# Experts over 13 tiles of 128 tokens instead of 14 of 112, two per-token values spread over the channels by DMA, and a new order of the work

## The reference

```
y   = layernorm over channels (x)                       # per token: (x - mean) * rstd
y   = spatial gate(y) * y                               # theta, phi, gram, joint, hidden, logit, sigmoid
y   = channel gate(y) * y                               # three products with 784-wide weights, gram, joint, sigmoid
x   = x + y
t   = x as tokens; tn = layernorm(t)
p   = softmax(tn @ router_w + router_b); top 2 of 8 experts, renormalised
t   = t + sum over the 2 of p_k * (tn @ expert_w[k] + expert_b[k])
out = t back as images
```

## Time and profile before

| | us |
|---|---|
| median of 3 runs | 2124.07 (2121.37 to 2126.17) |
| profiled execution, its own time | 2119.73 |
| its span, first to last instruction | 2117.9 |
| TensorE busy | 1966.1 |
| VectorE busy | 1602.6 |
| ScalarE busy | 1182.8 |
| GpSimd busy | 1041.1 |

### The profile page before, as it was taken

How to read it: one execution, slowest core, us unless ns; L and a number is a source line. 1 busy time by engine, 2 the same in 40 slices (tenths; PEclk the granted TensorE clock), 3 DMA queues, 4 the chain that set the end, 5 groups by cost and what they waited for, 6 DMA issues and landing times.

```text
span 2117.9 us, 41604 instructions
## 1 busy us (share of the span) xinstructions
PE 1966.1 (93%) x14484; PEld 1425.6 (67%) x14484; DVE 1602.6 (76%) x4919; ACT 1182.8 (56%) x3304; POOL 1041.1 (49%) x1233
## 2 busy tenths in 40 slices
PE   1689999999999999999999999999999999999986
PEld 1466677776677676667777667777666776766663
DVE  2457787887778787778788877878877788887775
ACT  1346555565655556665556565555666555556534
POOL 0225545555454554554455555455554545555544
PEclk9899999999999999999999999999999999999998
DMA  3000000000000000000000000000000000000000
GB/s 101 1 17 24 24 31 16 32 32 24 32 24 32 17 32 28 27 24 32 19 29 32 24 32 24 32 16 32 32 24 32 24 32 17 31 24 32 9 16 31
DMA packets 23707, 57.78 MB, mean 27 GB/s; under 512 B 5132, under 2 KB 6333, under 8 KB 23502
## 3 DMA queue, kind: packets, MB, share of 16 engines
q1 hardware_dynamic: 23502, 55.13, 7.4%
HBM read 29.43 MB, written 25.69 MB: 26 GB/s over the span
## 4 chain that ended last, share of the span: by engine, by line
PE 63%; DVE 18%; issue 12%; ACT 5%; SPq 1%; POOL 1%; DMA 0%; DVEq 0%; POOLq 0%; ACTq 0%
DVE part L1419 5%; PE high L1019 5%; ACT part L625 5%; PE rot L771 5%; PE low L1019 4%; PE rot L844 4%; PE high L1021 4%; PE rot L824 4%; PE high L1020 4%; PE low L1021 4%; PE low L1020 3%; PE rot L763 3%; PE rot L756 3%; PE rot L857 2%; PE rot L794 2%
## 5 line engine op out<-in xcount | busy, mean ns | idle before, releaser
L625 ACT ACTIVATE part<-low,gv 112x128 f32<-112x128 f32 x1792 | 500.9, 392 | 277.8 <-issue 134.3
L426 POOL TENSOR_TENSOR part<-part 112x256 f32<-112x256 f32 x448 | 344.8, 770 | 474.5 <-DVE part L1419 474.2
L1419 DVE SCALAR_TENSOR_TENSOR part<-high,gv,part 112x128 f32<-112x128 f32 x1792 | 493.7, 342 | 110.5 <-ACT part L625 97.4
L888 PE MATMUL rot<-x1h,wch 112*128 112x256 f32 x1120 | 280.9, 289 | 6.5 <-ACT x1h L564 6.5
L889 PE MATMUL rot<-x1h,wcl 112*128 112x256 f32 x1120 | 269.4, 279 | 0.0
L431 POOL TENSOR_TENSOR otok<-part 112x128 f32<-112x128 f32 x448 | 208.0, 464 | 35.1
L417 POOL TENSOR_TENSOR x1l<-tok,x1h 112x1024 fp32r<-112x1024 f32 x64 | 135.7, 2121 | 175.3 <-ACT x1h L564 175.3
L1019 PE MATMUL low<-weh,xh 128*112 128x512 f32 x448 | 196.8, 439 | 25.7 <-ACT part L625 23.1
L888 PEld LDWEIGHTS rot<-x1h,wch 112*128 112x128 f32 x1120 | 211.6, 189 | 12.9 <-ACT x1h L564 12.6
L889 PEld LDWEIGHTS rot<-x1h,wcl 112*128 112x128 f32 x1120 | 211.9, 189 | 0.0
L387 POOL TENSOR_TENSOR rstd<-var,mhalf 112x14 f32<-112x14 f32 x32 | 85.2, 2662 | 255.1 <-DVE var L1219 255.1
(11 more groups left out here) (204 smaller groups left out, 3903.6 us busy)
## 6 DMA issues: line engine op xcount, KB each, us to landing
xin<-in_x SPq DMA_DIRECT2D x32, 784.0 KB, 4.3
out<-x SPq DMA_DIRECT2D x64, 392.0 KB, 2.3
otok<-in_ggs_w SPq DMA_DIRECT2D x1, 600.2 KB
y_ch<-in_ggs_w SPq DMA_DIRECT2D x1, 600.2 KB
j<-in_expert_w SPq DMA_DIRECT2D x1, 512.0 KB
x<-in_thc_w SPq DMA_DIRECT2D x1, 392.0 KB
x<-in_phc_w SPq DMA_DIRECT2D x1, 392.0 KB
x<-in_gxc_w SPq DMA_DIRECT2D x2, 183.8 KB
```

The costliest lines, as they stand in the source:

```text
L426: nc.gpsimd.tensor_tensor(part[:, slot, 0:2, :], part[:, slot, 0:2, :], part[:, slot, 2:4, :], ALU.add).then_inc(sem("half_sum"), 1)
L625: last = nc.scalar.activation(part[:, slot, e, :], low[i % 2][0:T, e * C:(e + 1) * C], ACT.Copy, scale=gv[o][:, i, e:e + 1])
L888: nc.tensor.matmul(dst, wch[:, j, rows], hi_x, start=(j == 0), stop=False)
L1419: last = nc.vector.scalar_tensor_tensor(out=part[:, slot, e, :], in0=high[i % 2][0:T, e * C:(e + 1) * C], scalar=gv[o][:, i, HALF + e:HALF ...
```

## The change

**Tiles.** The second half cuts a pair's 1568 tokens without regard to the border of the images: 12 tiles of 128 tokens and one of 32 (`TILES` is 13), in four pieces of three, three, three and four tiles (`FLAT`). Statistics, shift, routing, gates, expert halves, token sums and `finish` all go by these tiles and pieces. The first half keeps its tiles of 112. An expert tile's PSUM bank and its slot in `part` now go by a running count over all pairs, since 13 is odd.

**Spreading by DMA.** Instead of 14 transposes of a broadcast column, one transpose turns the values of all tiles to rows (14 x 112 or 13 x 128), ScalarE copies them to SBUF, SP writes them to a row in DRAM, waits for that, and reads the row back into all 128 partitions of `y_ch` or `cen`. `normalise` and `centre` then work in place: both operands lie in SBUF.

**Order.** The lists of all engines, and `USES`, are new. Among others `mixed` and its copies move to the next step (back 1), `x_tokens`, `stats1`, `moments1` and `centre_tokens` move to the early part of the step, nine tiles of gating (4 to 12) come ahead of `x1_tokens`, `normalise` comes right behind `x1_tokens`, and the routing behind that.

```diff
+TILES = -(-PAIR * S // 128)
+FLAT = ((0, 3), (3, 6), (6, 9), (9, TILES))
...
+                def row_out(name, src, back):
+                    if live(k, p, back):
+                        need(sp, f"{name}_row_ready", k, p, 1, back)
+                        sp.dma_start(rows_dram[name][turn(back) % 2], src[:, :]).then_inc(sem(f"{name}_row_out"), 16)
+                def row_in(name, dst, back):
+                    if live(k, p, back):
+                        sp.wait_ge(sem(f"{name}_row_out"), 16 * (turn(back) + 1))
+                        sp.dma_start(dst, rows_dram[name][turn(back) % 2].rearrange("i t -> (i t)")[0:PAIR * S].partition_broadcast(128))\
+                          .then_inc(sem(f"{name}_spread"), 16)
...
                 load(0)
+                shift_out(2)
+                shift_in(2)
+                rstd_out(0)
+                rstd_in(0)
                 store(0, 3)
                 store(1, 3)
...
+                def rstd_turn(back):
+                    if live(k, p, back):
+                        free(pe, "rstd_row", k, p)
                         need(pe, "rstd1_ready", k, p, 1, back)
-                        spread(f"scale{b}{q}", rstd1[par(p, back)], b, q, back).then_inc(sem("scale_filled"), 1)
+                        nc.tensor.transpose(bank("rstd_row", k, p, back)[0:2 * NT, 0:T], rstd1[par(p, back)][:, :], ident[0:T, 0:T])\
+                            .then_inc(sem("rstd_row_filled"), 1)
...
-                        need(dve, "scale_filled", k, p, 2 * b + q + 1, back)
-                        nc.vector.tensor_tensor(y_ch[:, b, cols(q)], bank(f"scale{b}{q}", k, p, back)[:, 0:width(q)],
-                                                x[par(p, back)][:, b, cols(q)], ALU.mult).then_inc(sem("y_ch_ready"), 1)
+                        dve.wait_ge(sem("rstd_spread"), 16 * (2 * k + p - back + 1))
+                        own = y_ch[:, b, cols(q)]
+                        nc.vector.tensor_tensor(own, own, x[par(p, back)][:, b, cols(q)], ALU.mult).then_inc(sem("y_ch_ready"), 1)
...
+                def centre(f, back):
+                    if live(k, p, back):
+                        dve.wait_ge(sem("shift_spread"), 16 * (2 * k + p - back + 1))
+                        own = flat(cen)[:, span(f)]
+                        nc.vector.tensor_tensor(own, flat(x2[par(p, back)])[:, span(f)], own, ALU.subtract)\
                             .then_inc(sem("centred_ready"), 1)
```

More of the change, by code:

```diff
@@ L229, in need, with rows, span, flat @@
             eng.wait_ge(sem(name), k * (2 * PER[name]) + ((p - back) * PER[name] + n))
+        def rows(i):
+            return min(128, PAIR * S - 128 * i)
+        def span(f):
+            return slice(128 * FLAT[f][0], min(128 * FLAT[f][1], PAIR * S))
+        def flat(v):
+            return v[:, :, :].rearrange("p b s -> p (b s)")
+        def piece(i):
+            return min(i // 3, 3)
+        def count_of(k, p, back, i):
+            return (2 * k + p - back) * TILES + i
         def ago(i, d, back):
@@ L1006, in router, with finish @@
                         last.then_inc(sem("rlogit_filled"), 1)
-                def finish(b, q, back):
+                def finish(f, back):
                     if live(k, p, back):
-                        free(pe, f"fin{b}{q}", k, p)
-                        need(pe, "token_ready", k, p, NT * b + QUART[q][1], back)
-                        to_channels(f"fin{b}{q}", otok, b, q, back).then_inc(sem("fin_filled"), 1)
-                def products(dst, o, i, half):
-                    b, j = i // NT, i % NT
-                    tile = slice(j * T, (j + 1) * T)
+                        free(pe, f"fin{f}", k, p)
+                        need(pe, "token_ready", k, p, FLAT[f][1], back)
+                        for i in range(*FLAT[f]):
+                            n = rows(i)
+                            last = nc.tensor.transpose(bank(f"fin{f}", k, p, back)[:, (i - FLAT[f][0]) * 128:][:, 0:n],
+                                                       otok[0:n, i, :], ident[0:n, 0:n])
+                        last.then_inc(sem("fin_filled"), 1)
@@ L1046, in step @@
+                low_half(7, 3)
+                high_half(6, 3)
+                high_half(7, 3)
+                mixed(1)
+                x_tokens(0, 0, 0)
+                x_tokens(0, 1, 0)
+                x_tokens(1, 0, 0)
+                x_tokens(1, 1, 0)
+                high_half(8, 3)
                 joint(0, 0, 1)
-                x2_tokens(1, 1, 2)
-                low_half(7, 3)
-                high_half(7, 3)
+                joint(0, 1, 1)
+                high_half(9, 3)
+                finish(1, 3)
@@ L1097, in step @@
                 high_half(3, 2)
+                gram_first(1)
+                tp_tokens(0, 0)
+                low_half(2, 2)
+                gram_turn(1)
+                channels(2, 1)
                 joint_c(1)
-                scale(1, 0, 0)
-                scale(1, 1, 0)
                 high_half(4, 2)
                 hidden_c(1)
-                theta_phi(0, 0)
-                finish(0, 0, 2)
+                finish(0, 2)
+                low_half(3, 2)
+                channel_logit(1)
@@ L1441, in step @@
+                stats2(3, 2)
+                gate_high(6, 3)
+                moments2(2)
+                mix_low(1)
+                gate_high(7, 3)
+                stats1(0, 0)
+                shifts(2)
+                stats1(1, 0)
+                finish(1, 3)
+                moments1(0)
                 gate_high(8, 3)
+                centre_tokens(0, 0)
                 gate_high(9, 3)
-                shifts(2)
                 gate_high(10, 3)
-                centre(0, 0, 2)
-                centre(0, 1, 2)
```

503 lines of the change are left out of this document (247 added, 256 removed).

## The result

The changed kernel takes 2187.3 us (median of four runs, 2185.3 to 2190.1) against 2125.1 for the kernel before on the same chip: ratio 1.0295, 95% interval 1.0278 to 1.0312. Slower, as forecast and inside the range, but by 62 us where the forecast had 21.

The account below looks back on a forecast made before the run. TensorE bounds the kernel before; after the change a closed VectorE-TensorE circle does: 31.0 + 26.9 + 5.0 = 62.9 us a step against 62.44. 2119.7 + 13 (29 steps) + 12 (filling and draining) = 2145 us, range 2045 to 2190.

Parts of the forecast that it names:

- The closed chain: VectorE's new order and TensorE's channel products wait on each other in one circle; the step can't be shorter, 62.9 us.
- C: Circle from residual(1,1) to the first x1h: 29.6 us of work plus 1.3 of blocking by GpSimd, 31.0 (rounded up).
- A: Circle from channels0_high to the channel logit: 23.3 us work, 0.5 small waits, 3.1 waiting for normalise behind x1_low; 26.9.
- B: Circle from the channel logit to residual(1,1): one tile of gating, the gate and four residuals on VectorE, 5.0 us.
- What TensorE saves: Spreading transposes 2.99 us less 0.3, 14th tile 1.4, logits and token transpose 0.1: 4.2 a step, leaving 56.4.
- The first line of "what would show it": Normalise (448 columns) well above 0.55 us, its third piece ending 4 us or more after x1h(0).
- The second: Sign in the profile after: TensorE waits for normalise before theta_phi(0), about 3 us a step.
- The trips through DRAM: Each spread takes 6.6 us out and in, hidden under 8.9 us of cover for the shift, 10.6 for the deviation.
- Rival 3: The spread from one DRAM row is slow, 11 us out and in: step 65.0, 2214 us; chance 0.06.
- Filling: Uncovered trips at the start, 6.6 us each for the first pair's deviation and shift, within +12 for filling and draining.
- The draining: At the end, some 3 us in each of the two last shifts; about 7 credited for the saved tile and transposes.
- Rival 1: TensorE stays the bound, faster, 2056 us, if blocking in A and C together is below about 3.6 us; chance 0.37.

Follow-up runs that it names:

- hold_x1: The changed kernel with GpSimd's x1_low held until both x1_tokens are done: 2242.4 us, 1.0572 of the kernel before.
- no_x1low: The changed kernel with x1_low working on 8 columns only from the second pair on, leaving out the fine part of x1: 2074.7 us, 0.978 of the kernel before.
- tiles_only: The kernel before with only the 13 tiles of 128 tokens added, spreads still by TensorE transposes and lists in the old order: 2066.3 us, 0.9747.
- warm: The changed kernel with 22 unused matmuls of 256 columns a step filling TensorE's gap in channels0_high: 2154.0 us, 1.0151 of the kernel before.
- pool_after: hold_y with GpSimd's x_low(1) to x_low(3) moved behind x1_low, and gx(1) ahead of channels0_low on TensorE: 2183.4 us, 1.0291 of the kernel before.
- rstd_twice: The changed kernel with the DMA spread of the reciprocal deviation read twice, one after the other: 2195.1 us, 1.0353 of the kernel before.
- dma_old_order: 13 tiles and both spreads by DMA as in the change, but lists in the order of the kernel before: 2517.4 us, 1.1863 of that kernel.
- hold_y: The changed kernel with x1_low held until both x1_tokens and all of normalise are done: 2181.8 us, 1.0292 of the kernel before.
- swap_low: The changed kernel with x_low(3) ahead of add_token(12) in GpSimd's list: 2195.8 us, 1.0347 of the kernel before.
- split_low: The changed kernel with each x1_low issued as four and three instructions, back to back: 2209.1 us (two runs), 1.04 of the kernel before.

## Why the prediction was right in sign and wrong in size

**The closed chain: right.** No engine is the bound (TensorE 88%, VectorE 73%), and the step follows what lies on the circle: longer in hold_x1 (66.0), shorter in no_x1low (60.4). The parts, measured on the same marks: C 30.2 us (residual(1,1) ends at 1029.3, x1h(0) at 1059.5) for 31.0; A 28.4 (to the channel logit) for 26.9; B 5.35 for 5.0. Sum 63.95 for 62.9.

**What TensorE saves: right for the tile (1.5 us, tiles_only), too high in all.** It works 57.5 us a step in no_x1low where I had 56.4. tiles_only, with its spreads by transposes, has 59.1, so the two spreads gave back some 1.6 us where the sum had 2.7.

**Part C: near, by two errors.** centre lost less than the 1.3 assumed: 731 ns for 384 columns against 546 from PSUM in tiles_only, three times, 0.55 in all. GpSimd paid instead, x_low at 1344 ns against 1012. And "VectorE without waits from the statistics of x2 to the space gate" was wrong: it waits 0.89 us for ScalarE at 1045.5, and the chain of waits in the changed kernel runs over TensorE and ScalarE up to 1047.4 and over VectorE only from there.

**Part A is the step that failed.** The prediction put the block on normalise: "GpSimd is released to x1_low(0)" at the instant when VectorE is free for it, 3.1 us. It had VectorE free there "since x1_tokens(1) runs beside that copy", that is at its 0.95 us. The row of 2391 ns for this form was read as one GpSimd instruction's rest, and it was: before, GpSimd had x1_low(0) and then a gap. In the new list add_token(12) and x_low(3) run straight into x1_low(0), and x1_tokens(1) took 4.56 us; TensorE waited in channels0_high, 2.7 us, and normalise was free. By itself this wait is no longer than the one forecast. What was missing from the sum is what TensorE does after it: theta_phi(0) and gx(0) at half clock, 1.0 us in their two groups and 1.2 a step in all, about 31 us of the kernel (warm). This is the term that was put at nothing without a reason. The prediction had the clock at 1.00 throughout, as the earlier trace rows shows it, and did not ask what a wait of 3 us does to it. Without the term its step comes out: 62.7 us in warm, and 62.6 to 62.7 in the changed kernel's five full-clock steps, for 62.9 forecast. The first line of "what would show it" thus came out wrong: normalise takes 0.61 us, and its third piece ends 5.4 us after x1h(0) only because it starts late. The second came out nearly (2.7 us of wait, before another group), the third too (share 88% for 89, rest 5.2 us for 6.5).

The rule of the Trainium skill that the prediction weighed (SBUF — State Buffer, Who interferes with whom) says that a VectorE instruction with two SBUF inputs contends with a GpSimd instruction that reads SBUF. The trace agrees on x1_tokens (4.56 us beside GpSimd, 0.95 in pool_after without it). It does not say what happens when several GpSimd instructions follow each other, and that is what decided here.

**The trips through DRAM: hidden, as forecast, in the steady part.** Of 6.6 us assumed out and in, the trace shows the row out in 1.4 (issued 1049.35, the spread issued 1050.75) and the spread in 3.9. rstd_twice adds at most 0.4 us a step. Rival 3 is out. Their price is that they need the new order: in the old one the kernel takes 18.6% more than before (dma_old_order), and 22% more than tiles_only, from which it differs by the trips alone.

**Filling: +18.8 for +12, mis-sized.** VectorE waits 8.12 us for the first deviation and 3.36 for the first shift. But it waited for TensorE at these places before, too. The first normalise and the first space logit of the changed kernel, then of the kernel before:

```profile
79.46 2.00 DVE L1311 TENSOR_TENSOR y_ch<-y_ch,xin 128x448 f32<-128x448 f32 x4 [8.12 <-DMA y_ch<-rstd_rows]
109.50 0.29 DVE L1324 TENSOR_SCALAR sp<-rot,sbs 112x12 f32<-112x12 f32 x1 [6.69 <-PE rot L945]
```

```profile
73.98 1.07 DVE L1242 TENSOR_TENSOR y_ch<-rot,xin 128x448 f32<-128x448 f32 x2 [2.68 <-PE rot L771]
95.06 0.29 DVE L1256 TENSOR_SCALAR sp<-rot,sbs 112x12 f32<-112x12 f32 x1 [10.45 <-PE rot L876]
```

The first trip shows as 5.5 us. By the space logit the delay is 14.4, by the channel logit 16.7 (138.05 for 121.36), by the first centre, behind the second trip, 18.5 (158.06 for 139.55). So the two trips make some 7 us of the 18.8. The other 11 or so arise between them, where `mixed` now waits for the next step and the clock is 0.71 and 0.66 (80 to 100 and 100 to 120 us; before 1.00 and 0.91). No run separates these two. The sum had only the trips. The first gv of dma_old_order comes as late (178.6), by another road: in the old order the space logit is 6.3 us late and the channel logit 13.1. The draining that I charged with some 6 and credited with 7 came out at nothing (38.9 us in both).

**Sum.** 31 steps at 1.6 and 18.8 of filling are 68.7 where 13 + 12 stood. Of the 44 us between them (68.7 less 25) 37 lie in the step. In warm the same 31 steps take 1937.6 us, 32 less than in the changed kernel and 17.7 more than before, where 13 were forecast: that puts the clock at 32 of the 37.

Rival 1 (2056, faster) is near what the kernel does with most of the conflict gone: 2074.7. Its condition was a blocking below 3.6 us in A and C together. By the measured numbers (2.7 + 0.55 = 3.3 us) it was met, and the kernel was slower all the same, since the circle it was added to lacked 1.1 us of TensorE's work and the 1.2 of the clock. That the forecast beat this rival is in part luck.

**Where the gain went.** The change is two changes. The tiles give 2.5% (tiles_only). The DMA spreads, with the order they need, take some 1.6 us more off TensorE and cost all of it and more: even with most of the conflict gone (no_x1low, 2074.7) the kernel isn't faster than tiles_only (2066.3). Its step is 0.5 us shorter, but its first gv comes 13 us later (172.4 for 159.0). Of the three attempts to move the conflict (hold_y, pool_after, swap_low) none came below 1.029 of the time before: from x1_tokens to the end of the routing VectorE goes from one instruction with two SBUF operands to the next. The new order with both spreads by transposes was not tried, so what the order alone costs is open; it needs eight PSUM uses among four banks.

## What to carry to other kernels

When work moves from PSUM operands to SBUF operands on VectorE, list what GpSimd has queued at that moment without a gap: the price is the whole row of instructions, and moving the row only changes who pays while VectorE has such work throughout. When a forecast adds a wait of 2 to 3 us to TensorE in a kernel that ran at full clock, add what the matmuls behind it cost at half clock (here it fell after 14 of 19 such waits). Test the parts of a change one by one: here one half was worth 2.5% alone.

## What was not expected of the hardware

- A VectorE instruction that waits for GpSimd was passed over at every boundary of up to six GpSimd instructions (x1_tokens 4.98 us in split_low) and through two in the routing (3.85 us in hold_y). But the first piece of normalise in hold_x1 and swap_low came in between x1_low(0) and x1_low(1), which followed each other without a gap, and centre(2), started 0.2 us after an x_low, took 0.54 us while the x_low was stretched to 1.61. The runs don't show what decides. x1_tokens and the comparison have an operand that is repeated over columns (gain, mx), normalise and centre don't. That this decides is a guess, and no run separates it.
- GpSimd pays as well: x1_low(1) 3.13 us beside normalise for 1.84, add_token(12) 1.52 beside x1_tokens(0) for 0.45.
- TensorE, busy 92% of a step, fell to 1.2 GHz in 14 of 19 steps after it had waited 2.7 us at a stretch, and stayed at 2.4 GHz in the other five. In hold_x1 no wait for normalise is longer than 1.5 us, but there are two of them close together, and its mean clock is 0.946. In hold_y no wait is longer than 1.25 us; two of 1.1 and 1.0 us stand within 3 us of each other, and 0.50 follows in 13 of some 19 steps. In warm, no_x1low and tiles_only, with single waits of 1.2 us, the steady window shows 1.00.
- One 6 KB row of DRAM read into 128 partitions, 784 KB, takes 3.9 to 4.0 us, no more than a load of 784 KB from as many bytes of DRAM (4.3).
